# Two-layer attention and FFN kernel: output projection as products of rounded parts, weight quantisation and mask rows moved

## What is computed

```python
x = x + cross_attention(layernorm(x), ctx)       # 16 heads, latent queries and keys, rotary
x = x + fp8_ffn(layernorm(x), w_fc, w_proj)      # square(relu(.)), per-tensor scaled e4m3
x = x + gated_softmax(ctx, ctx, masks, layernorm(x))
x = x + routed_ffn(x)                            # rmsnorm, value/out projection, SwiGLU 256 -> 704
```

```python
attn = softmax(scores)                                  # 16 heads
ctx_c = einsum('bhsl,bld->bhsd', attn, kv_r)            # 64 per head
ctx_lat = einsum('bhsd,hkd->bhsk', ctx_c, w_kc_kv)
return ctx_lat.transpose(0, 2, 1, 3).reshape(B, S, H * K) @ Wo.T
# in the second layer
x8 = (x2d / scale_x).astype(float8_e4m3fn); w8 = (w / scale_w).astype(float8_e4m3fn)
```

## Time and profile before

| engine | busy us | share of the span | instructions |
|---|---|---|---|
| PE (matmul) | 362.0 | 96% | 2193 |
| PE (weight load) | 269.1 | 71% | 2193 |
| DVE | 293.1 | 78% | 674 |
| ACT | 207.2 | 55% | 555 |
| POOL | 174.2 | 46% | 163 |

### The profile page before, as it was taken

One profiled execution on the slowest core, in us unless ns is written; L12 is line 12 of the kernel. 1 busy time (PEld: TensorE's weight loads), 2 busy tenths in 40 slices (PEclk: granted clock), 3 DMA queues, 4 the chain that ended last, 5 costly groups with the idle time before them and its releaser, 6 DMA issues.

```text
span 376.8 us, 6340 instructions
## 1 busy us (share of the span) xinstructions
PE 362.0 (96%) x2193; PEld 269.1 (71%) x2193; DVE 293.1 (78%) x674; ACT 207.2 (55%) x555; POOL 174.2 (46%) x163
## 2 busy tenths in 40 slices
PE   8899999999999999999999999998999999989996
PEld 8775776777677767876767587864557567779885
DVE  5698698698668786986796656578899988896773
ACT  1524576566647664865575495616975371682240
POOL 2453765486458546754765440581711042146000
PEclk9999999999999999999999999999999999999999
DMA  7639100300301203000004000400000000000101
GB/s 230 237 114 336 77 1 2 111 3 1 114 0 17 96 2 112 3 0 2 0 1 155 2 1 0 124 0 1 2 1 2 0 2 1 0 2 2 40 16 56
DMA packets 9086, 17.53 MB, mean 47 GB/s; under 512 B 2144, under 2 KB 6944, under 8 KB 8160
## 3 DMA queue, kind: packets, MB, share of 16 engines
q1 hardware_dynamic: 9056, 17.14, 13.5%
HBM read 16.09 MB, written 1.05 MB: 45 GB/s over the span
## 4 chain that ended last, share of the span: by engine, by line
PE 67%; DVE 14%; POOL 9%; ACT 4%; issue 3%; DMA 2%; SPq 0%; DVEq 0%; POOLq 0%
PE bank L1523 15%; PE bank L1564 8%; PE bank L1582 7%; PE bank L1573 6%; PE bank L1607 4%; PE bank L1548 4%; POOL prob L463 4%; PE bank L1533 3%; PE bank L1476 3%; PE bank L1827 2%; DVE relu L1159 2%; PE bank L1443 2%; DMA blobs<-in_blob 2%; POOL rot_low L458 2%; PE bank L1444 2%
## 5 line engine op out<-in xcount | busy, mean ns | idle before, releaser
L463 POOL TENSOR_TENSOR prob<-prob,rinv 128x512 f32<-128x512 f32 x64 | 66.0, 1042 | 78.4 <-DVE rinv L1023 78.4
L1523 PE MATMUL bank<-xnT,w 128*128 128x512 f32 x288 | 83.1, 425 | 1.7 <-DVE xnT L920 1.7
L621 ACT ACTIVATE prob<-bank,negmax 128x256 f32<-128x256 f32 x128 | 59.7, 488 | 29.5 <-DVE negmax L1017 29.5
L1017 DVE TENSOR_REDUCE negmax<-bank 128x2 f32<-128x512 f32 x64 | 40.9, 681 | 37.7 <-PE bank L1564 37.7
L1523 PEld LDWEIGHTS bank<-xnT,w 128*128 128x128 f32 x288 | 52.4, 188 | 22.0 <-issue 13.3
L631 ACT COPY probT<-bank 128x512 f32<-128x512 f32 x64 | 35.2, 592 | 23.6 <-PE bank L1573 23.6
L951 DVE TENSOR_TENSOR rot_up<-bank,cb 64x512 f32<-64x512 f32 x64 | 44.1, 689 | 1.6
L458 POOL TENSOR_TENSOR rot_low<-rot_low,rot_up 128x512 f32<-128x512 f32 x32 | 41.0, 1282 | 3.8 <-DVE rot_up L951 3.8
L443 POOL TENSOR_TENSOR c_y<-c_ve,minus_half 128x4 f32<-128x4 f32 (+1 forms) x9 | 9.8, 1087 | 57.8 <-DVE c_ve L901 45.5
L1573 PE MATMUL bank<-ca,prob 128*128 128x128 f32 x256 | 34.2, 273 | 0.3 <-POOL prob L463 0.3
L1573 PEld LDWEIGHTS bank<-ca,prob 128*128 128x128 f32 x256 | 30.1, 140 | 5.3 <-POOL prob L463 0.8
(11 more groups left out here) (212 smaller groups left out, 702.7 us busy)
## 6 DMA issues: line engine op xcount, KB each, us to landing
blobs<-in_blob SPq DMA_DIRECT2D x7, 1024.0 KB, 4.8
xs<-in_x SPq DMA_DIRECT2D x2, 512.0 KB, 4.0
xn<-in_w_fc_t SPq DMA_DIRECT2D x1, 1024.0 KB, 4.9
ctxT<-in_w_proj_t SPq DMA_DIRECT2D x1, 1024.0 KB, 5.4
out<-qk SPq DMA_DIRECT2D x8, 128.0 KB, 1.7
cb<-in_const_b SPq DMA_DIRECT2D x1, 768.0 KB, 8.5
blobs<-in_w_gate SPq DMA_DIRECT2D x1, 704.0 KB, 5.7
blobs<-in_w_up SPq DMA_DIRECT2D x1, 704.0 KB, 7.1
```

The source lines that it names most:

```text
L463: pool.tensor_tensor(p[:], p[:], rinv[:, n % PROBS, :].unsqueeze(2).to_broadcast([P, 2, S]), ALU.mult).then_inc(normed, 1)
L621: ins = act.activation(prob[n % PROBS][:, st, :], pS[n % UNITS][:, st * S:(st + 1) * S], ACT.Exp, bias=negmax[:, n % UNITS, st:st + 1], ac ...
L1017: dve.tensor_reduce(negmax[:, n % UNITS, :], pS[n % UNITS][:].rearrange("p (a s) -> p a s", a=2), AX, ALU.max, negate=True).then_inc(max_r ...
L1523: ins = pe.matmul(q_bank(m)[:], w[a][:, k, r * P:(r + 1) * P], x[b][:, k, c * CH:(c + 1) * CH], start=(i == 0), stop=(i == 5))
```

## The change

- `project_ahead(n)` becomes three matmuls of rounded parts by `product`. The eight of the last pair stay float32 matmuls.
- `wkvo` is rounded by ACT (`wkvo_round`) in rounds 10 (pairs 0 to 3) and 12 (pairs 4 to 6); DVE makes the rest in place (`wkvo_rest`).
- `cT` is rounded by ACT and DVE in fourteen pieces of 128x512 (`cT_round(f, c)`, `cT_rest(f, c)`), written out in round 14: five ahead of its context copy, two among its exponentials, seven among its turned copies. On DVE two of the rests stand between the inverse sums and the last maximum. The rounded parts lie where queries and their weights were.
- The eight pieces of w8 come behind all of these in round 14, on ACT and on DVE.
- POOL does `power(3)` first, then mask rows 0; rows 1 now wait for `x8_ready` with rows 2 and 3.

```diff
@@ POOL
-            for b in range(2):
-                mask_rows(b)
             power(3, c_ve[:], minus_half[:], c_y[:])
+            mask_rows(0)
             pool.wait_ge(x8_ready, NT // 2)
-            for b in range(2, B):
+            for b in range(1, B):
                 ins = mask_rows(b)
@@ ACT
+            def wkvo_round(i):
+
+                act.wait_ge(wkvo_ready, WK_CUT[i])
+                act.copy(wkvo_high[:, wk_part(i), :], wkvo[:, wk_part(i), :]).then_inc(wkvo_rounded, 1)
+
+            def cT_round(f, c):
+
+                act.wait_ge(q_ready, ALLQ)
+                act.wait_ge(u_ready, 2 * (GROUPS - 2) + 1)
+                act.wait_ge(cT_copied, 2 * f + c + 1)
+                act.copy(cT_high[c * (PAIRS - 1) + f], cT[:, f, c * CH:(c + 1) * CH]).then_inc(cT_rounded, 1)
...
             n = UNITS * QUIET
+            for f in range(5):
+                cT_round(f, 0)
             context_copy(QUIET - 1)
             exponentials(n)
             exponentials(n + 1)
-            w8_cast(0)
+            cT_round(5, 0)
+            cT_round(6, 0)
             exponentials(n + 2)
             u_copy(QUIET + 1)
             turned_probs(n)
             exponentials(n + 3)
-            w8_cast(1)
+            cT_round(0, 1)
             turned_probs(n + 1)
-            w8_cast(2)
+            cT_round(1, 1)
+            cT_round(2, 1)
             turned_probs(n + 2)
-            w8_cast(3)
+            cT_round(3, 1)
+            cT_round(4, 1)
             turned_probs(n + 3)
-            for j in range(4, W8_PIECES):
+            cT_round(5, 1)
+            cT_round(6, 1)
+            for j in range(W8_PIECES):
                 w8_cast(j)
@@ DVE
+            def wkvo_rest(i):
+
+                dve.wait_ge(wkvo_rounded, i + 1)
+                dve.tensor_tensor(wkvo_rests[:, wk_part(i), :], wkvo[:, wk_part(i), :], wkvo_high[:, wk_part(i), :].bitcast(F32),
+                                  ALU.subtract).then_inc(wkvo_low, 1)
+
+            def cT_rest(f, c):
+
+                dve.wait_ge(cT_rounded, c * (PAIRS - 1) + f + 1)
+                cols = slice(c * CH, (c + 1) * CH)
+                dve.tensor_tensor(cT_rests[:, f, cols], cT[:, f, cols], cT_high[c * (PAIRS - 1) + f].bitcast(F32),
+                                  ALU.subtract).then_inc(cT_low, 1)
...
             n = UNITS * QUIET
+            for f in range(5):
+                cT_rest(f, 0)
             largest_score(n)
             largest_score(n + 1)
             largest_score(n + 2)
             inverse_sum(n)
+            cT_rest(5, 0)
             largest_score(n + 3)
+            cT_rest(6, 0)
             inverse_sum(n + 1)
-            w8_round(0)
             inverse_sum(n + 2)
             inverse_sum(n + 3)
-            for j in range(1, W8_PIECES):
+            for f in range(PAIRS - 1):
+                cT_rest(f, 1)
+            for j in range(W8_PIECES):
                 w8_round(j)
@@ PE, in project_ahead
-                project(t, f)
+                if t == 0:
+                    pe.wait_ge(wkvo_low, 1 + (f >= WK_CUT[0]))
+                c, at = t // B, t % B * P
+                pe.wait_ge(cT_low, c * (PAIRS - 1) + f + 1)
+                product(bank[OUT_BANK[t // 2]][:, t % 2 * D:(t % 2 + 1) * D],
+                        (cT_high[c * (PAIRS - 1) + f][:, at:at + P], cT_rests[:, f, t * P:(t + 1) * P]),
+                        (wkvo_high[:, f, :], wkvo_rests[:, f, :]), f == 0 and t % 2 == 0, False)
```

More of the change, by code:

```diff
@@ L51 @@
 WD_ROUNDS = (7, 9, 11)
+WK_CUT = (4, 7)
+WK_ROUNDS = (10, 12)
 LARGEST_ROUNDS = (1, 3)
@@ L189, in build @@
             probT += [part(f"probT_{i}", [P, 2, S], F32) for i in range(2, UNITS)]
+            part("apart", [P, 3 * D], F32)
+            wkvo_high = part("wkvo_high", [P, PAIRS - 1, D])
+        with ExitStack() as rest_only:
+            cT_rests = rest_only.enter_context(nc.sbuf_tensor("cT_rests", [P, PAIRS, TOK], F32R))
+            wkvo_rests = rest_only.enter_context(nc.sbuf_tensor("wkvo_rests", [P, PAIRS, D], F32R))
+            rest_only.enter_context(nc.sbuf_tensor("between", [P, 11 * TOK], F32))
+            cT_more = rest_only.enter_context(nc.sbuf_tensor("cT_more", [P, 2, CH], F32R))
         ctxn = prob[PROBS - 1][:].rearrange("p a s -> p (a s)").rearrange("p (t d) -> p t d", t=NT)
@@ L274, in build @@
         wkvo_ready = sem("wkvo_ready")
+        wkvo_rounded, wkvo_low, cT_rounded, cT_low = (sem(n) for n in
+                                                      ("wkvo_rounded", "wkvo_low", "cT_rounded", "cT_low"))
         turned_high = sem("turned_high")
@@ L333, in q_bank, with wk_part @@
             return bank[Q_BANK[m]] if m < QSTEPS else pq[m % 2]
+        cT_high = [xnT[i][:, k, c * CH:(c + 1) * CH] for i in range(2) for k in range(DK) for c in range(2)]
+        cT_high += [w1[j][i][:].rearrange("p a b -> p (a b)")[:, 0:CH] for j in range(2) for i in range(2)]
+        cT_high += [cT_more[:, r, :] for r in range(2)]
+        def wk_part(i):
+            return slice(WK_CUT[i - 1] if i else 0, WK_CUT[i])
         def rots(n):
@@ L680, in _ @@
                     wd_round(WD_ROUNDS.index(g))
+                if g in WK_ROUNDS:
+                    wkvo_round(WK_ROUNDS.index(g))
             n = UNITS * QUIET
+            for f in range(5):
+                cT_round(f, 0)
             context_copy(QUIET - 1)
@@ L1076, in _ @@
                     wd_part(WD_ROUNDS.index(g))
+                if g in WK_ROUNDS:
+                    wkvo_rest(WK_ROUNDS.index(g))
             n = UNITS * QUIET
+            for f in range(5):
+                cT_rest(f, 0)
             largest_score(n)
@@ L1603, in last_contexts, with project @@
                     context_of(GROUPS - 1, a, last_pV[a][:, 0:S]).then_inc(pv_ready, 1)
-            def project(t, f):
-                return pe.matmul(bank[OUT_BANK[t // 2]][:, t % 2 * D:(t % 2 + 1) * D], cT[:, f, t * P:(t + 1) * P],
-                                 wkvo[:, f, :], start=(f == 0 and t % 2 == 0), stop=(f == PAIRS - 1 and t % 2 == 1))
+            def project(t):
+                return pe.matmul(bank[OUT_BANK[t // 2]][:, t % 2 * D:(t % 2 + 1) * D],
+                                 cT[:, PAIRS - 1, t * P:(t + 1) * P], wkvo[:, PAIRS - 1, :], start=False,
+                                 stop=(t % 2 == 1))
             def project_ahead(n):
@@ L1627, in project_last @@
                 for t in (2 * i, 2 * i + 1):
-                    ins = project(t, PAIRS - 1)
+                    ins = project(t)
                 ins.then_inc(attn_ready, 1)
```

## The result

The changed kernel took 385.88 us (median of four runs, 381.91 to 386.36); the kernel before, run beside it, 379.75 (378.50 to 380.87). The ratio is 1.0154, 95% interval 1.0122 to 1.0187: slower, 1.2 us above the forecast and within its range. The profiled execution took 385.85 us with a span of 384.1; before it was 379.05 and 376.8. So the time around the span went from 2.25 to 1.75; no run shows why, and it makes differences of spans 0.5 larger than those of times. The mean granted clock of the four runs was 0.987, 0.996, 0.987 and 0.987, in the order of 385.85, 381.91, 385.90 and 386.36 us.

What follows compares the result with a forecast made beforehand. PE was taken as nearly always busy but tied to the softmax chain, with 2.84 us of DVE slack; 1.7 + 2.4 + 0.7 = +4.8 on 379.05 gave 383.85, plus 0.88 to the median, 384.7; range 381.6 to 387.0.

Steps and rivals of the forecast that it cites:

- the likeliest case: Whole kernel: 384.7 us, with its own bounds 383.3 to 385.8; chance 0.50.
- rival (c): TensorE's clock halves after its waits for unit 60 and in the Newton stretch: 1.9 us more, 386.6; chance 0.14.
- (b): Newton step escapes the stretch by POOL's scaling of bytes, the rest holds: +2.4, 382.3 us; chance 0.18.
- What the products save: Projections: 0.359 us for three products against 0.431; 4.0 us of PE time in all, 0.72 behind turn 63.
- Round 14: Attention: five differences contend with POOL's join, adding 1.0; first maximum at 215.2, turn 59 at 225.3 against 224.16.
- The quantisation: Eight late w8 pieces hold round 15's first maximum until 239.4, 3.9 later; unit 60 turned at 242.6, +2.8.
- Rival (d): Quantisation hides ahead of round 15's first maximum and PE's 4.0 us come through whole: 375.9; chance 0.05.
- The end of the attention: Attention ends 1.7 us later; bounds 0.6 without contention, 2.0 with the join's full length.
- Mask rows 0: Behind POOL's power, its scaling and addition stretch two Newton operations on DVE: +2.4 us, bounds 0 and 2.76.
- Scale of h: POOL's later wgu_rest holds DVE's two small multiplications to 277.5 instead of 276.8: +0.7 us, bounds 0 and 1.0.

Runs made afterwards that it cites:

- the filled kernel: Changed kernel with unread matmuls in PE's waits: ahead of turn 60, after the last residual, ahead of the second sum over partitions; 381.64 us, ratio 1.0060.

## Why the prediction was right or wrong

The direction, the range and nearly the number were right; the sum behind it was not. It put 4.8 us on queues and sharing. These took 2.2 to 2.5 in time (2.8 by the spans, 379.6 against 376.8), and the clock, which the forecast had left to a rival, 4.1. Two errors of opposite sign nearly met, and that is luck. There is a third part of luck: between the two profiled executions lie 6.8 us (385.85 and 379.05), 2.0 more than the sum; the forecast hid 0.9 of this by starting from the median of before, 0.88 above its profiled execution. The measured 385.88 is 0.1 above the upper bound that I gave the likeliest case (the bounds of its three terms, added to 379.93, give 380.5 to 385.7, so the 383.3 there has no working), and nearest to rival (c), 386.6, yet what happened is (b) and (c) together, which I had not listed: 382.3 with two falls.

- **What the products save.** Right: 0.36 a projection. At full clock turn 63 to the last residual takes 9.00 in the filled kernel (246.39 to 255.39), 9.62 before (243.73 to 253.35): 0.62 against the 0.72 forecast.
- **Round 14.** Right. The first maximum at 215.18 (said 215.2); five differences beside the join took 4.18, 1.1 above 0.69 and four steps of 0.60 (said 1.0). Turn 59 at 225.33 (said 225.3).
- **The quantisation.** Right: first maximum of round 15 at 239.50 with no idle in front (said 239.4), turn 60 at 242.62 (said 242.6). Rival (d) falls with this.
- **The end of the attention.** 3.27 later in the changed kernel, 2.0 in the one with its waits filled, whose fill itself delayed turn 60 by 0.1. Said: 1.7. The remainder is the first fall, which took 1.3 between turns 60 and 63.
- **Mask rows 0: one of the two steps that failed.** Said +2.4, measured +0.34. The term had DVE held twice, each time to the end of POOL's instruction. The addition's hold is real (1.15 beside 1.26) but comes too late to matter; the scaling's ended early, 0.63 into its 1.50. The row I went by the earlier trace rows was one of float additions; of a scaling of bytes beside DVE there was no row, which is what rival (b) rested on, and the term should have stood nearer to the middle of its bounds. Nor is it only a matter of width, as the prediction had it: the scaling is as wide as the addition. The whole move of the mask rows costs 1.0 at full clock. The Trainium skill, "SBUF — State Buffer", SBUF: two separate sides, has the lock last for the whole instruction. By that the first operation would have ended at 261.85; the trace says 260.98.
- **Scale of h.** Right in kind and size: the two small multiplications took 0.52 and 0.38, ending at 280.62 and 281.03, the second with POOL's last float subtraction (281.02), and PE's sum over the partitions is 4.15 later than before where the pad was 3.65 later: +0.5 (said 0.7).
- **The clock: the other.** The sum left it out. Rival (c) had the mechanism for the attention and nearly its price in one fall (said 1.9; 1.3 measured), at a chance of 0.14; the clock of all eight runs of the changed kernel was below 1.000, in seven of them at 0.987 or less. It did not have the second fall, 2.7 and its tail of 0.6. It said "some 3 us" of gap in the Newton stretch; PE's longest waits there are 0.95 and 1.08, and the clock stayed at 1.000. The Trainium skill, "TensorE: Matmul & The Clock Gate", Part 1, names an idle TensorE as what brings the clock down. The first fall agrees, after a wait of 3.35. Ahead of the second, from 266.2 to 284, no wait of PE is longer than 0.86, so one long wait is not its cause.

What stays open: what brings the second fall. PE waited 0.86 us for the sum in the changed kernel and 0.84 in the one filled in the attention only, both with the fall; it waited 0.82 with the mask rows moved alone, without it. In single profiles the fall was gone with the old mask order, half as large with the wait for unit 60 filled, and gone with all fills. But with the old mask order and the two differences moved, the clock fell from 256 to 268 instead, so the mask order does not settle it, and the fills behind the attention were not tried alone on this kernel. Nor is it known why kernels so alike have falls at different places (240 to 248; 220 to 228; 256 to 268).

## What to carry to other kernels

A faster TensorE pays only up to the slack of the chain it waits for; here 4.0 us of PE's time were saved with casts and differences that used up 2.84 us of DVE's slack and 4.0 more. When an edit makes PE wait, price the clock beside the wait, and test it with matmuls that nobody reads: if the kernel gets faster by doing more while the granted clock comes back, it was the clock. Look at how many runs keep the full clock, not at one profile alone. Sort runs by their mean clock before explaining a microsecond: one run in three of the kernel before had a lower mean, and took 1.4 more.

## What the runs showed of the hardware that was not expected

- A DVE operation with two SBUF operands and eight columns took 0.17 alone, 0.16 beside POOL's power of eight columns, 0.51 when it began 0.12 behind the start of POOL's scaling of 512 bytes a partition (1.50), and 1.15 when it began 0.13 behind that of a float addition of 512 columns (1.26), with whose end it ended.
- In 25 of 75 runs of a kernel in which PE's longest wait behind the attention is 1.1 us, the mean granted clock was 0.991 to 0.995 and the time 1.4 longer; in none of twelve when matmuls filled these waits (5 of 23 beside them).
- Matmuls in one wait of 3.35 us took away 4.0 us of time (385.88 to 381.89), of which the fall right behind that wait explains 1.3. The fall 40 us later was half as large in the profile, and missing in four runs of ten.
- The second fall of the changed kernel cost more than the first, as it lasted longer (3.4 against 1.7 us of full-speed clock): the 64 matmuls of 256 columns of the second FFN took 8.87, where before they took 7.15.
